# Four graph layers on one core: layer 2's own rows two tiles ahead, the second attention's normalization without a centred row

## The reference

```
L0: e = leaky((Wh1_i + Wh2_j)/sqrt(N)); softmax over neighbours; attention @ Wh; norm per node; + h; elu
L1: 4 heads: scores h h^T, softmax, attention @ h; leaky; @ Wo -> h2
    second attention: scores h2 h2^T, softmax, attention @ h2 + bo; z = leaky(..., 0.2)
    out = (z - mean(z)) * rsqrt(var(z) + 1e-5) * gamma + beta
L2: scores leaky(q k^T, 0.01), softmax; attention @ (h W)
L3: e = leaky(e_i + e_j); softmax; attention @ h; relu
```

## Time and profile before

| | us |
|---|---|
| median of 3 runs | 1559.11 (1558.41 to 1561.33) |
| the profiled execution | 1559.02 |
| its span, first to last instruction | 1557.2 |
| busy: DVE / POOL / PE / ACT | 1252.0 / 1014.2 / 921.7 / 791.9 |
| second attention, first softmax ended to last row ready | 917.6 to 1166.7 |
| L2, first softmax ended to last row staged | 1180.2 to 1386.1 |

### The profile page before, as it was taken

One profiled execution on the slowest core, in us unless ns is written; L12 is line 12 of the kernel. 1 busy time (PEld: TensorE's weight loads), 2 busy tenths in 40 slices (PEclk: granted clock), 3 DMA queues, 4 the chain that ended last, 5 costly groups with the idle time before them and its releaser, 6 DMA issues.

```text
span 1557.2 us, 15741 instructions
## 1 busy us (share of the span) xinstructions
PE 921.7 (59%) x4155; PEld 616.8 (40%) x4155; DVE 1252.0 (80%) x1592; ACT 791.9 (51%) x2666; POOL 1014.2 (65%) x965
## 2 busy tenths in 40 slices
PE   1137564761678676468788856567515546656581
PEld 0014332320456565357676622222205546642230
DVE  7889586996899999999999449989857996856461
ACT  2025444667165565355767824457683565652230
POOL 2132388621898897659898868877547875448881
PEclk9999886985799999879999987787757787878796
DMA  9951477421222231101120044523115633247665
GB/s 340 227 206 60 121 205 194 144 70 59 87 58 83 68 101 48 48 7 41 42 61 28 15 142 142 142 88 108 35 44 180 180 114 108 69 140 209 183 202 146
DMA packets 101571, 176.83 MB, mean 114 GB/s; under 512 B 47489, under 2 KB 56225, under 8 KB 99425
## 3 DMA queue, kind: packets, MB, share of 16 engines
q0 software_dynamic: 31472, 102.93, 22.7%
q1 hardware_dynamic: 67280, 72.13, 14.8%
q10 hardware_dynamic: 2720, 0.68, 0.2%
HBM read 145.78 MB, written 34.10 MB: 116 GB/s over the span
## 4 chain that ended last, share of the span: by engine, by line
DVE 53%; POOL 19%; issue 10%; ACT 6%; PE 6%; DMA 4%; DVEq 0%; POOLq 0%; ACTq 0%; SPq 0%
DVE big L1783 14%; DVE big L1775 11%; POOL big L693 10%; POOL big L720 5%; ACT big L993 3%; DVE big L1779 3%; DVE big L1724 2%; PE PS L1358 2%; DVE big L1667 2%; DVE big L1603 2%; DVE big L1729 1%; DMA big<-in_adj 1%; DVE big L1767 1%; PE PS L1339 1%; DVE stats L1700 1%
## 5 line engine op out<-in xcount | busy, mean ns | idle before, releaser
L993 ACT ACTIVATE big<-big 128x64 f32<-128x64 f32 x1496 | 371.1, 339 | 155.1 <-DVE big L1740 144.3
L720 POOL TENSOR_TENSOR big<-big 128x512 f32<-128x512 f32 x373 | 377.5, 1043 | 70.2 <-DVE big L1740 65.9
L1358 PE MATMUL PS<-ident,big 128*128 128x128 f32 x1740 | 246.0, 305 | 143.8 <-ACT big L1102 64.1
L1783 DVE TENSOR_REDUCE big<-big 128x32 f32<-128x2048 f32 (+4 forms) x126 | 297.6, 2362 | 4.3
L1358 PEld LDWEIGHTS PS<-ident,big 128*128 128x128 f32 x1740 | 226.9, 160 | 160.3 <-ACT big L1102 68.7
L1339 PE MATMUL PS<-big,ident 128*128 128x512 f32 x348 | 190.7, 707 | 119.8 <-ACT big L993 75.7
L693 POOL DMA_INDIRECT big<-tab,SI x142 | 179.2, 1262 | 75.5 <-issue 40.6
L1775 DVE TENSOR_TENSOR big<-big,PS 128x2048 f32<-128x2048 f32 (+4 forms) x84 | 198.5, 2363 | 18.2 <-PE PS L1370 15.3
L693 POOL DMA_INDIRECT big<-h_rows,SI x142 | 137.5, 969 | 51.2 <-issue 27.9
L1339 PEld LDWEIGHTS PS<-big,ident 128*128 128x128 f32 x348 | 76.3, 227 | 224.1 <-issue 201.7
L1355 PE MATMUL PS<-big,ident 128*128 128x512 f32 x174 | 113.5, 818 | 64.6 <-POOL big L720 64.6
(11 more groups left out here) (181 smaller groups left out, 1628.5 us busy)
## 6 DMA issues: line engine op xcount, KB each, us to landing
big<-in_adj SPq DMA_DIRECT2D x16, 1024.0 KB, 6.1
tab<-big SPq DMA_DIRECT2D x64, 132.0 KB, 1.8
big<-tab SPq DMA_DIRECT2D x32, 264.0 KB, 3.6
h_rows<-big SPq DMA_DIRECT2D x32, 256.0 KB, 2.0
big<-h_rows SPq DMA_DIRECT2D x32, 256.0 KB, 2.8
big<-in_x SPq DMA_DIRECT2D x16, 256.0 KB, 5.2
big<-xs SPq DMA_DIRECT2D x4, 1024.0 KB, 9.0
h_table<-big SPq DMA_DIRECT2D x16, 256.0 KB, 2.0
```

Source lines behind the costliest of these rows:

```text
L720: ins = pool.tensor_tensor(bd(wbuf[:, i % NWB, j, :]), bd(rows[:, k + j, :]), over_d(S[:, h, k + j, :], B), ALU.mult)
L993: ins = act.activation(to, row, ACT.Copy, scale=S[:, h, k + j, b:b + 1])
L1358: mm = pe.matmul(to[:, q * P:(q + 1) * P], wbuf[:, i % NWB, k, q * P:(q + 1) * P], ident[:, :], start=(first and q == 0), stop=(last and q ...
L1783: run(dve.tensor_reduce(scores(u, t)[:, h, k:k + n, :].rearrange("p k b -> p (k b)"), bd(prod[:, 0:n * E]), AX.X, ALU.add))
```

## The change

In the second attention the row is not centred any more. The mean is kept with its sign turned; ScalarE squares the row itself with that as a bias, eight operations per tile, each giving its sum; VectorE multiplies the turned mean by the root (`nshift`, new semaphore `z_shift`), and ScalarE scales with nshift as bias. GpSimd's subtraction and VectorE's sum of squares go. ScalarE's copy of the sum, the logarithm and the root move to the head of its iteration. For the last three tiles (`LATE = 3`) VectorE does the scaling, in two operations, and also ends the layernorm's row in one operation (`end_norm`) in place of ScalarE's eight.

In L2 the own row is turned at m for tile m+2 (was m+1), and ScalarE takes it near the end of its iteration; the copy of the sum comes straight after the weighing; the product, the addition to X and all that follows them come one iteration sooner (m-2 for m-3, and so on). TensorE's order is: query, turn next, halves, turn own, product, sum. VectorE's is: variance, ending, addition, mean.

```diff
-for m in range(-1, NT + 10):
-    for what, t in (("own", m + 1), ("next", m - 6)):
+for m in range(-2, NT + 10):
+    for what, t in (("next", m - 5), ("own", m + 2)):
...
-                                store_halves(3, m - 7)
+                                store_halves(3, m - 6)
...
                 def finish2(m):
-                    t = m - 3
-                    if 0 <= t < NT:
-                        pool.wait_ge(z_mean, t + 1)
-                        pool.tensor_tensor(bd(no[:, t % 4, :]), bd(no[:, t % 4, :]),
-                                           over_d(ln[:, 0, (t % 2) * B:(t % 2 + 1) * B], B), ALU.subtract)\
-                            .then_inc(z_centred, 1)
...
                             if u == 3:
-                                centre(3, m - 4)
+                                centre(3, m - 3)
...
-                        if l < 3:
+                        if l < 3 and not (l == 2 and s - 1 >= NT - LATE):
...
                 for m in range(NT + 10):
-                    weigh(2, m - 1, 0)
+                    t = m - 2
+                    if 0 <= t < NT:
+                        act.wait_ge(chunk_summed, last_chunk(2, t) + 1)
+                        if t >= 4:
+                            act.wait_ge(x1_added, t - 3)
+                        act.activation(no[:, t % 4, :], bank(t % 2), ACT.Relu, scale=0.8).then_inc(o_relu, 1)
                     t = m - 4
...
                         act.activation(ln[:, 1, v], ln[:, 3, v], ACT.Exp, scale=-0.5).then_inc(z_rooted, 1)
-                        act.wait_ge(z_rooted, t + 1)
+                    weigh(2, m - 1, 0)
+                    if 0 <= t < NT - LATE:
+                        act.wait_ge(z_shift, t + 1)
                         for b in range(B):
                             part, i = no[:, t % 4, b * D:(b + 1) * D], (t % 2) * B + b
-                            ins = act.activation(part, part, ACT.Copy, scale=ln[:, 1, i:i + 1])
+                            ins = act.activation(part, part, ACT.Identity, scale=ln[:, 1, i:i + 1],
+                                                 bias=nshift[:, i:i + 1])
                         ins.then_inc(o_scaled, 1)
                     t = m - 3
                     if 0 <= t < NT:
-                        act.wait_ge(z_centred, t + 1)
-                        if t >= 2:
-                            act.wait_ge(z_var, t - 1)
-                        act.activation(na[:, t % 2, :], no[:, t % 4, :], ACT.Square).then_inc(z_squared, 1)
+                        act.wait_ge(z_mean, t + 1)
+                        for b in range(B):
+                            i = (t % 2) * B + b
+                            ins = act.activation(na[:, t % 2, b * D:(b + 1) * D], no[:, t % 4, b * D:(b + 1) * D], ACT.Square,
+                                                 bias=ln[:, 0, i:i + 1], accum_out=ln[:, 2, i:i + 1])
+                        ins.then_inc(z_var, 1)
                     norm(2, m - 6)
-                    t = m - 2
-                    if 0 <= t < NT:
-                        act.wait_ge(chunk_summed, last_chunk(2, t) + 1)
-                        if t >= 4:
-                            act.wait_ge(x1_added, t - 3)
-                        act.activation(no[:, t % 4, :], bank(t % 2), ACT.Relu, scale=0.8).then_inc(o_relu, 1)
                     exp(2, m)

-                for m in range(-1, NT + 10):
-                    if 0 <= m + 1 < NT:
-                        if m + 1 >= 2:
-                            act.wait_ge(q_made, 3 * NT + m)
-                        take_turned(hTo[:, (m + 1) % 2, :])
+                for m in range(-2, NT + 10):
                     weigh(3, m - 1, 0)
-                    norm(3, m - 4)
                     t = m - 2
                     if 0 <= t < NT:
                         act.wait_ge(chunk_summed, last_chunk(3, t) + 1)
...
                         act.activation(aT[:, t % 2, :], bank(0), ACT.Copy).then_inc(aggT_made, 1)
-                    if 0 <= m - 6 < NT:
-                        if m - 6 >= 2:
-                            act.wait_ge(half_projected, 2 * (NT + m - 6 - 1))
-                        take_turned(hT3[:, (m - 6) % 2, :])
-                    halves(3, m - 7, (0, 1))
+                    norm(3, m - 3)
+                    s = m - 5
+                    if 0 <= s < NT:
+                        if s >= 2:
+                            act.wait_ge(half_projected, 2 * (NT + s - 1))
+                        take_turned(hT3[:, s % 2, :])
+                    halves(3, m - 6, (0, 1))
+                    if 0 <= m + 2 < NT:
+                        if m + 2 >= 2:
+                            act.wait_ge(q_made, 3 * NT + m + 1)
+                        take_turned(hTo[:, m % 2, :])
                     exp(3, m)
...
                 for u in (2, 3):
                     for m in range(NT + 10):
                         divide(u, m - 1)
+                        t = m - 4
+                        if u == 2 and 0 <= t < NT:
+                            v = slice((t % 2) * B, (t % 2 + 1) * B)
+                            dve.wait_ge(z_rooted, t + 1)
+                            if t >= 2:
+                                dve.wait_ge(o_scaled, t - 1)
+                            tell(dve.tensor_tensor(nshift[:, v], ln[:, 0, v], ln[:, 1, v], ALU.mult), z_shift, t + 1)
+                            if t >= NT - LATE:
+                                o = no[:, t % 4, :]
+                                run(dve.tensor_tensor(bd(o), bd(o), over_d(ln[:, 1, v], B), ALU.mult))
+                                tell(dve.tensor_tensor(bd(o), bd(o), over_d(nshift[:, v], B), ALU.add), o_scaled, t + 1)
                         if m < NT:
                             rows_here(u, m)
...
                         if u == 2:
                             finish2(m)
                         else:
-                            t = m - 3
+                            variance(3, m - 3)
+                            end_norm(3, m - 4)
+                            t = m - 2
                             if 0 <= t < NT:
                                 dve.wait_ge(z_made, NT * HEADS + t + 1)
                                 tell(dve.tensor_tensor(X[:, t, :], bank(6), X[:, t, :], ALU.add), sum_used, NT + t + 1)
-                            norm(3, m - 3)
+                            row_mean(3, t)
```

More of the change, by code:

```diff
@@ L262, in program @@
         ln = sb("ln", [P, 4, 2 * B])
+        nshift = sb("nshift", [P, 2 * B])
         epsc = sb("epsc", [P, 1])
@@ L1694, in near, with row_mean @@
                 dve.wait_ge(info_loaded, 16)
-                def norm(l, s):
+                def row_mean(l, s):
                     if 0 <= s < NT:
@@ L1829, in finish2 @@
                         tell(dve.tensor_tensor(X[:, t, :], no[:, t % 4, :], X[:, t, :], ALU.add), x1_added, t + 1)
[L1830 to L1835 removed]
+                    row_mean(2, m - 5)
+                    variance(2, m - 6)
+                    if m - 7 >= NT - LATE:
+                        end_norm(2, m - 7)
                     t = m - 2
@@ L1850, in near @@
                     elu_add(m - 5)
-                    norm(1, m - 5)
+                    row_mean(1, m - 5)
+                    variance(1, m - 6)
                     elu_low(m - 4)
```

63 lines of the change are left out of this document (31 added, 32 removed).

## The result

Before 1558.76 us, after 1541.80 us (medians of four runs each; 1557.81 to 1561.33 and 1540.65 to 1545.62). The ratio is 0.989, 95% interval 0.987 to 0.991: faster, by 17 us (1.1%) and not by the 28 of the forecast. On another chip the same pair gave 0.990 (0.988 to 0.993). The profiled execution took 1542.32 us, its span is 1540.6 (1557.2 before).

The account below looks back on a forecast made before the run. VectorE bounds both stages' starts; in layer 2's second half the queue order does; ScalarE becomes the late iterations' bound. Second attention -15.9 and layer 2 -12.2 sum to -28.1: 1559.11 to 1531 us, likeliest 1526 to 1536, range 1516 to 1550.

Parts of the forecast that it names:

- two rivals (1540 and 1542): Squares at 4.3 us a tile: 1540, chance 0.17; layer 2's sums end a chain, returning 11 us: 1542, 0.12.
- (e): Second attention: VectorE's nshift meets the start of GpSimd's run in late iterations and waits for one L720, 1.0 us.
- The rival for the slower side: Second attention: nshift waits for GpSimd's whole run, 6.2 us per late iteration; kernel 1566, chance 0.07.
- (g): Second attention, ScalarE: one 0.62 us square becomes eight with bias and sum, 3.3 us a tile (2.0 to 4.3).
- (f): Second attention, ScalarE: the scaling gets a bias pointer, 76 ns per operation, 0.6 us per tile.
- Way out -4.2: Second attention's tail: last row ready 35.8 us after the last softmax instead of 40.0, with VectorE ending three tiles.
- L2 behind the widest tile: Layer 2's second half: 89.7 us falls to 78.6, with VectorE's work, joints and a few waits left.
- The ring: Layer 2's second half: TensorE's sum waits 32.7 us for ScalarE's copy, ScalarE 27.3 for TensorE's turn behind that sum.
- L2's start +1, way out -2.1: Layer 2: early extra VectorE work +3, less one stall, +1 net; tail of 20.9 us falls to 18.8.
- Layer 2 keeps most of its time: Behind the wide tile TensorE's sums end a chain within the iteration, taking 11 us again: 1542, chance 0.12.
- Cheap squares: Second attention: squares take 2.0 us a tile, so VectorE bounds the late iterations; kernel 1521, chance 0.15.
- The signs of being wrong: Squares outside 2.0 to 4.3 us; nshift of 5; VectorE idle over 8 behind layer 2's widest tile; tail not under 40.

Follow-up runs that it names:

- nshift_split: The changed kernel with nshift of tiles 0 to 12 on GpSimd and of the last three on VectorE: 1535.12 us, ratio to before 0.9829.
- pool_steps: The changed kernel with a semaphore wait between GpSimd's operations in the second attention: 1533.88 us in a single run (kernel before 1563.16 on that chip).
- nshift_pool: The changed kernel with all nshift computed by GpSimd ahead of its weighings: ratio to before 0.9866.

## Why the prediction came out as it did

The sign was right, and so was ScalarE as the bound of the late iterations. The gain was over-estimated by 11 us: 1541.8 lies inside the range of 1516 to 1550, outside the 1526 to 1536 held likeliest, and next to the figures of two rivals (1540 and 1542) whose mechanisms did not come. The step that failed is in (e), the price of nshift: "late runs begin out of idleness". It accounts for 4 of the 11 us directly; L2's stretches add 5.6 more and the start of the second attention 1.9.

- **(e), six late iterations: -3.1 forecast, +1.0 measured.** "I take one L720, 1.0 us, since late runs begin out of idleness." For three of the six that held (0.91 to 0.97 us), two more met nothing. One run did not begin out of idleness: at iteration 10 the gathers behind the widest tile end 0.02 us before it, and the root came 0.80 us late, so nshift met the whole run, 6.99 us. The idle time there had been 1.02 us, and the change takes 1.05 us more of work from GpSimd; together that is less than the 2.6 us by which the forecast itself shortened the iteration ahead of it. The row that the forecast leaned on, at 1036.02, was of the kernel before. The rival for the slower side had priced just that wait, in every iteration; it came once in the late ones. Taking it out gave 5.9 us (nshift_split). The forecast had the late root as "cost about 0.3 us, on VectorE only", since the sum that the copy reads is an iteration old; the 13-row tile's sum is not finished by then, and that lateness put nshift behind the start of the run.
- **The rule weighed there** (Trainium skill, SBUF — State Buffer, "Who interferes with whom": the lock is held for one whole instruction) would have given one L724 at most. The traces disagree where a run has no pause: 6.99 us over seven instructions. With a semaphore pause at each boundary they agree: no wait past the instruction that ran or was about to start. As far as the runs here go, the rule holds where GpSimd's run has pauses or begins out of idleness.
- **ScalarE as the new bound: right, and cheaper than thought.** ScalarE's busy time rose from 55.7 to 71.9, forecast 75.4. (g) squares: 3.3 us a tile taken, 2.74 measured: one pair of square and read-out each 0.33 us, inside the forecast's 2.0 to 4.3. (f) The bias pointer: 425 ns for L1078 against 335, 90 ns and not 76. By the Trainium skill (ScalarE: Activation LUTs, "What ACT_TABLE_LOAD costs") a pointer adds about 93 ns; the trace agrees to 3 ns.
- **VectorE's waits in the late iterations:** 7.5 us were to fall away; L1733 and L1738 still have some 1.4 us, so 6.1 did, and L1896 added 9.2 us over its own 1.0.
- **Start of the second attention: -6 forecast, -4.1.** VectorE's busy time did fall by 7.0 us (105.5 to 98.5), its waits for GpSimd included: 3.5 us shorter for the 3 taken, with one nshift in them that waited for four L724 (3.65 us at 943.98). Its idle time grew by 2.8. That VectorE alone ends this stretch, as the sum supposed, is not borne out: in pool_steps 5.5 us less of it did not move the end.
- **Widest tile -2.6:** measured -2.4. Right.
- **Way out -4.2, measured -4.7: near by luck.** The forecast was for the last row of the second attention, 35.8 us after the last softmax for 40.0. It came after 33.7 (1157.6), so -6.2: more than forecast. From that row to L2's first softmax it then took 15.1 us for 13.5, the wait for the third own row, which the forecast of L2 did not have.
- **L2 behind the widest tile: -11.1 forecast, -9.0.** The ring was the bound and is open. The wait behind the 13-row tile is 3.4 us at L1712 and not 2 at the addition. The 0.45 us over of L1749 in seven iterations are there as forecast; but taking them away gave 0.3 us, so as a term of the sum they were no price at all: ScalarE's chain of the norm stood behind them. The "about 3.5" of joints were 8.2 us in which VectorE was idle (72.5 busy of 80.7), 4.4 of them the wait at L1712.
- **L2's start +1, way out -2.1:** measured +2.5 and 0. The first iterations cost 2.1, 1.9 and 1.4 us more than before, and the iteration with the stall gave back 2.8. The last row is stored only 0.4 us sooner after the last softmax (20.5 us for 20.9; forecast 18.8), and the first gathers of the next stage wait for that store. In kernels with the same L2 it is 19.2 to 21.7 us, so the forecast's walk along the queues was too short in all of them; which step of it was not tried.
- **The rivals.** "Layer 2 keeps most of its time" did not come: 9.0 of the 11.1 us did. "Cheap squares" was near on the squares (2.74, between 2.0 and the 3.3 taken), but its mechanism did not come: with the long wait out ScalarE still bounds the late iterations (72.12 of 74.59), and that kernel stands at 1535.
- **The signs of being wrong.** Two of the four came, both narrowly or once: an nshift of 5 us (6.99, at one place), and VectorE idle for more than 8 us behind L2's widest tile (8.2). The squares stayed in their range, and the tail was shorter than 40 us.

## What to carry to other kernels

A small VectorE product of two SBUF inputs, placed right behind the instruction that releases a run of GpSimd operations, costs what the run makes of it: give it to GpSimd ahead of the run (measured: 5.9 us), or put a semaphore pause between GpSimd's operations, which lengthens GpSimd's chain; both together gave less than the first alone. Time that a change saves on one engine can take away the idle time by which another wait was short, so ask what the shorter iteration now meets. Look at each iteration and not at the mean: one of six held the whole shortfall of its stretch. A wait that is seen in a profile is worth nothing by itself; the one removed from L2's division came back as a wait for a root, and at the start of the second attention 5.5 us less of VectorE changed nothing. And compare a forecast with the end point that it was made for: the way out agreed only because two misses met.

## What the runs showed of the hardware

How long a VectorE operation with two SBUF inputs waits for GpSimd depends on whether GpSimd's run has a pause. Without one, and begun directly behind gathers (11 to 22 ns, or with a memset in front), it is nearly always the rest of the run: 6.99 and 7.06 us over seven operations, 3.65 over four. In the second attention and L2 of the twelve profiled executions without pauses it happened 35 times that such an operation began with at least two of the run's still to end; 34 waits ended within 0.1 us of the run's last operation, the other one operation earlier (nshift_pool, 960.14). Begun out of idleness, it was the rest of one operation. With a semaphore wait between the operations it never outlasted, in the second attention, the operation that ran or was about to start (1.34 us at most), at some 0.1 us per operation of GpSimd's pace (3.30 us for three L727, 5.03 for five L724 without). Why idleness ahead of a run without pauses has the effect of one is open.

A VectorE product with one input in PSUM took its usual 3.35 us beside five such GpSimd operations. A ScalarE square with a sum taken out shows as two instructions, 332 and 186 ns, one pair each 0.33 us; the plain scaling of the kernel before had one operation each 0.25 us (12.1 us for 48). TensorE's 128x512 float32 matmuls of the sum started 0.86 us apart at a granted clock of 0.51 and 0.43 us apart at 1.00 (1029.5 to 1043.0 in the changed kernel).
